# A transformer block on one core: one ring of Q and K for row maxima and logits, and a last half tile packed with gate and up

## The reference, cut to what matters

```
x  = x + layernorm(attn(layernorm(x)))
x  = x + layernorm(ffn(layernorm(x)))

attn: q, k, v = h @ Wq, h @ Wk, h @ Wv        # rotary on q and k
      attn = softmax(where(causal, q @ k.T, -1e9) / 8)
      out  = (attn @ v) @ Wo
ffn:  W = NF4[codes] * scales                  # for gate, up and down
      out = (silu(x @ Wg.T) * (x @ Wu.T)) @ Wd.T
```

## Time and profile before

| | |
|---|---|
| median of three runs | 2897.58 us |
| the profiled execution | 2898.06 us |
| span of its records | 2896.3 us |
| PE busy | 2703.1 us (93%) |
| DVE busy | 2119.8 us (73%) |
| ACT busy | 1815.4 us (63%) |
| POOL busy | 605.2 us (21%) |
| granted TensorE clock, mean | 0.98 |

### The profile page before, as it was taken

How to read it: one execution, slowest core, us unless ns; L and a number is a source line. 1 busy time by engine, 2 the same in 40 slices (tenths; PEclk the granted TensorE clock), 3 DMA queues, 4 the chain that set the end, 5 groups by cost and what they waited for, 6 DMA issues and landing times. The chain is left out here.

```text
span 2896.3 us, 54385 instructions
## 1 busy us (share of the span) xinstructions
PE 2703.1 (93%) x19792; PEld 1477.9 (51%) x19792; DVE 2119.8 (73%) x3538; ACT 1815.4 (63%) x2467; POOL 605.2 (21%) x399
## 2 busy tenths in 40 slices
PE   3999999989999999859979999999999999999996
PEld 1544444458888888725534444444444444444442
DVE  6975666568777878336657887887788788788886
ACT  3713334369999999822247767676766767776652
POOL 0100000068888888801120000000000000000011
PEclk9999999989999999979989999999999999999998
DMA  4353322143232332032211111111111111111124
GB/s 146 112 171 109 80 82 72 52 131 81 61 81 65 82 82 68 6 120 84 88 58 55 49 52 52 52 52 51 53 44 52 52 52 52 52 52 48 55 82 166
DMA packets 88664, 213.83 MB, mean 74 GB/s; under 512 B 14032, under 2 KB 18512, under 8 KB 88144
## 3 DMA queue, kind: packets, MB, share of 16 engines
q1 hardware_dynamic: 88400, 210.36, 23.8%
HBM read 174.59 MB, written 35.72 MB: 73 GB/s over the span
## 5 line engine op out<-in xcount | busy, mean ns | idle before, releaser
L1509 PE MATMUL gp<-region,wgu 128*128 128x512 f16 x4224 | 919.7, 380 | 5.9 <-DVEq L1609 3.3
L435 ACT ACTIVATE dequant<-dequant,offsets 128x512 f32<-128x512 f32 x992 | 659.3, 713 | 89.6 <-DVE dequant L464 45.6
L1509 PEld LDWEIGHTS gp<-region,wgu 128*128 128x128 f16 x4224 | 413.5, 98 | 507.2 <-issue 11.4
L966 POOL TENSOR_TENSOR pt_pair<-probs,pt_pair 128x1024 f16<-128x1024 f32 (+1 forms) x256 | 522.9, 2073 | 117.7 <-ACT probs L1113 117.4
L1524 PE MATMUL yp<-wd,inter 128*128 128x512 f16 x2112 | 465.6, 380 | 17.2 <-DVE wd L482 10.5
L290 DVE TENSOR_REDUCE mx<-sx 128x1 f32<-128x512 f32 (+3 forms) x640 | 363.3, 604 | 87.8 <-PE sx L280 57.0
L390 POOL TENSOR_TENSOR st<-st,eps 128x1 f32<-128x1 f32 x64 | 24.4, 381 | 1751.5 <-DVE st L1217 1511.0
L1108 ACT ACTIVATE pt_pair<-st,coef 128x1024 f16<-128x1024 f32 (+1 forms) x320 | 321.8, 1006 | 58.1 <-PE st L1035 53.8
L464 DVE TENSOR_TENSOR dequant<-dequant 128x512 f32<-128x512 f32 x496 | 341.1, 688 | 10.0
L1524 PEld LDWEIGHTS yp<-wd,inter 128*128 128x128 f16 x2112 | 205.9, 98 | 271.5 <-DVE wd L482 13.0
L806 PE MATMUL pq<-region,ht 128*128 128x512 f16 x1536 | 338.0, 379 | 3.0 <-DVEq L858 3.0
(11 more groups left out here) (123 smaller groups left out, 3256.7 us busy)
## 6 DMA issues: line engine op xcount, KB each, us to landing
qk_pairs<-r_pair SPq DMA_DIRECT2D x128, 128.0 KB, 2.3
k<-qk_pairs SPq DMA_DIRECT2D x48, 256.0 KB, 5.3
dequant<-in_down_codes SPq DMA_DIRECT2D x44, 256.0 KB, 3.0
dequant<-in_down_scales SPq DMA_DIRECT2D x88, 128.0 KB, 3.2
dequant<-in_gate_codes SPq DMA_DIRECT2D x40, 256.0 KB, 2.9
dequant<-in_gate_scales SPq DMA_DIRECT2D x80, 128.0 KB, 3.1
dequant<-in_up_codes SPq DMA_DIRECT2D x40, 256.0 KB, 2.9
dequant<-in_up_scales SPq DMA_DIRECT2D x80, 128.0 KB, 3.2
```

Source lines behind the costliest of these rows:

```text
L435: a.activation(line[:, k % 4, :], code7, ACT.Identity, scale=slope, bias=offsets[:, k:k + 1]).then_inc(s_L.sem, 1)
L966: eng.tensor_tensor(pt_pair[:, n0(u, g) % PT_RING, 1, 0:w], probs[:, n0(u, g) % P_RING, 0:w], pt_pair[:, n0(u, g) % PT_RING, 0, 0:w], ALU. ...
L1509: mm = pe.matmul(gp[:, e % 2, m, :], wgu[par][:, m, a, col0:col0 + P], xnT[:, b, k, tok], start=(k == 0 and a == b), stop=(k == KT - 1 and ...
```

## The change

It has three parts.

1. **Attention.** `q1`, `k1` and the two slots of `xq`, `xk` become one ring of three slots, head mod 3, which the maxima and the logits both read. The whole of head 0 is readied in the Q and K block: its maxima as before, and now also `turn_max`, the conversion (`shifted`), `spread_max`, and the loads of `q2`, `k2`; the three small operations for `shift` move there too, and POOL writes the constant rows of `k2[0]` there. SP's wait for the last stores moves into the attention block, behind the load of head 1's ring slot; POOL waits for them as well before it writes the constant rows of `k2[1]`. The attention block begins with the logits of head 0 (y = 28); the maxima of head 1 begin at y = 30, with 4 in the first slot and 3 in each of twelve more, those of head 2 take 17 slots (3, 2, 2, ...), the others two per slot as before. A head's ring slot is loaded when the logits of the head three before it are done.
2. **The packed half tile.** In the last group the second tile has only 64 real units. Its 64 gate and 64 up columns are placed side by side in one tile, so `gate_up` of that tile is 24 matmuls and not 48, and its `down` takes 2 matmuls and not 3 (the high and the low half of the product lie in the two halves of the partitions). The group before writes gate and up weights in this layout (`short_places`, up units with two instructions each on ACT and DVE); two of the down units are loaded twice over (`doubled`). ACT copies the gated half tile twice. The loop has one turn less: groups 8, 9 and 10 are straight code.
3. **GpSimd's addition of x1.** `output` moves from DVE to POOL, x1 has a ring of four rows loaded three ahead, and the scaled rows `yn` lie in a buffer of the dequantisation that is free by then.

```diff
+        RING = 3
+        FIRST_SLOTS = [4] + [3] * 12
+        SECOND_SLOTS = [3, 2, 2] * 5 + [3, 2]
...
+        y = XLEAD + 2
+        for head in range(1, HEADS):
+            counts = {1: FIRST_SLOTS, 2: SECOND_SLOTS}.get(head, [len(p) for p in per_slot])
+            k = 0
+            for n in counts:
+                maxima_in[y] = [(head, i) for i in range(k, k + n)]
+                k, y = k + n, y + 1
+            turn_in[y] = head
...
-            for y in range(NGH, last_lag):
-                slot(look(0, y))
-            for t in range(HEADS // 2):
-                for y in range(last_lag, last_lag + PAIR):
-                    slot(look(t, y))
+            for y in range(XLEAD, XLEAD + LAG_PV + HEADS * NGH):
+                slot(y, at_slot(y))
...
+                load_ring(sp, 1)
+
+                for u in range(2):
+                    sp.wait_ge(d_qk.sems[u], d_qk.done(KT))
+                load_low(sp, 1)
+                for head in range(HEADS):
+                    if head:
+                        spread_max(sp, head)
                         sp.wait_ge(s_S.sem, s_S.room(head * NGH))
+                    if head + 2 < HEADS:
+                        load_ring(sp, head + 2)
+                    if head and head + 1 < HEADS:
+                        load_low(sp, head + 1)
...
-            with eng.Fori(0, (NG - 1) // 2) as it:
+            with eng.Fori(0, (NG - 3) // 2) as it:
                 for par in range(2):
-                    body(it * 2 + par, par, False)
-            body(NG - 1, (NG - 1) % 2, True)
+                    body(it * 2 + par, par, False, False)
+            for g in range(NG - 3, NG):
+                body(g, g % 2, g == NG - 1, g == NG - 2)
...
+                            if last and t == 1:
+                                for k in range(KT):
+                                    col0 = k * GW + P
+                                    for a, b in ((0, 0), (0, 1), (1, 0)):
+                                        mm = pe.matmul(gp[:, 1, 0, :], wgu[par][:, 0, a, col0:col0 + P],
+                                                       xnT[:, b, k, tok], start=(k == 0 and a == b),
+                                                       stop=(k == KT - 1 and a == 1))
+                                mm.then_inc(s_u.sem, 1)
+                                continue
...
+                                    if last and t == 1:
+                                        for b in range(2):
+                                            mm = pe.matmul(yp[:, d % 4, :], inter[:, c % 2, 0, 1, j * P:(j + 1) * P],
+                                                           wd[:, b, E + n * CH:E + (n + 1) * CH],
+                                                           start=False, stop=(b == 1))
+                                        continue
...
+                for i in range(ST):
+                    pool.wait_ge(s_var6.sem, s_var6.done(i))
+                    inverse_root(pool, st6[:, i % 2, :], s_eps6, s_root6, i)
+                    if i:
+                        output(i - 1)
+                output(ST - 1)
```

More of the change, by code:

```diff
@@ L284, in piece, with maximum @@
             mm.then_inc(s_X.sem, 1)
-        def maximum(v, banks, head, u, k):
+        def maximum(v, banks, head, k):
             qt, c = items[k]
@@ L417, in dequant_buffers, with load_unit @@
             return cst, sst, line, below, above, code7
-        def load_unit(sp, buffers, n, slot, m, g, q):
+        def load_unit(sp, buffers, n, slot, m, g, q, doubled=False):
             cst, sst = buffers[0:2]
@@ L423, in load_unit @@
             cols = slice(q * CH, (q + 1) * CH)
+            if doubled:
+                for half in range(2):
+                    rows = slice(half * BLOCK, (half + 1) * BLOCK)
+                    sp.dma_start(cst[rows, slot, :], codes[m][g, 0:BLOCK, cols]).then_inc(d_st.sems[slot], 16)
+                sp.dma_start(sst[:, slot, :], scales[m][g:g + 1, 0, cols].to_broadcast([P, CH])
+                             ).then_inc(d_st.sems[slot], 16)
+                return
             sp.dma_start(cst[:, slot, :], codes[m][bass.ds(g, 1), :, cols].rearrange("a p c -> p (a c)")
@@ L790, in _ @@
                                 sp.wait_ge(d_qk.sems[which], d_qk.done(1))
-                            load_max(sp, 0, 0)
-                for u in range(2):
-                    sp.wait_ge(d_qk.sems[u], d_qk.done(KT))
+                            load_ring(sp, 0)
+                            load_low(sp, 0)
+                        if (t, u) == (KT - 1, 0):
+                            spread_max(sp, 0)
+            @block.gpsimd
+            def _(pool):
+                pool.memset(k2[0][D:P, :], GUARD).then_inc(s_guard.sem, 1)
             @block.tensor
@@ L1015, in slot @@
                         low_halves(pool, *z)
-                slots(pool, slot)
+                slots(slot)
             @block.tensor
@@ L1081, in times_v, with slot @@
                         mm.then_inc(s_PV.sem, 1)
-                def slot(at):
-                    x, turn, z, w = at(0), at(1), at(XLEAD), at(XLEAD + LAG_PV)
+                def slot(y, at):
+                    z, w = at(XLEAD), at(XLEAD + LAG_PV)
                     if z:
                         scores(*z)
-                    if turn and turn[2] == NGH - 1:
-                        turn_max(turn[0], turn[1])
-                    todo = per_slot[x[2]] if x else []
+                    if y in turn_in:
+                        turn_max(pe, sx, turn_in[y])
+                    todo = maxima_in.get(y, [])
+                    first = (len(todo) + 1) // 2
                     for half in range(2):
-                        if half < len(todo):
-                            item(x[0], x[1], todo[half])
+                        for head, k in todo[first:] if half else todo[:first]:
+                            item(head, k)
                         if w:
@@ L1095, in _ @@
                 pe.wait_ge(s_unset.sem, s_unset.done(1))
-                pe.wait_ge(s_guard.sem, s_guard.done(1))
-                slots(pe, slot)
+                slots(slot)
             @block.scalar
@@ L1558, in weight_high @@
                             a.wait_ge(s_u.sem, s_u.done(g * EVS + (-1)))
+                        if short_next and r >= UNITS:
+                            for unit, hi, _ in short_places(r, par):
+                                op = a.activation(hi, unit, ACT.Copy, scale=col(wfac, G_ + m))
+                            op.then_inc(s_whi.sem, 1)
+                            return
                         a.activation(hi_out, work[3][:, r % 2, :], ACT.Copy, scale=col(wfac, G_ + m)
@@ L1607, in _, with body @@
             def _(v):
[L1608 removed]
+                for s in (s_it, s_ilo, s_add):
                     v.sem_inc(s.sem, s.credit)
[L1610 removed]
+                def body(g, par, last, short_next):
                     def add(c, k):
```

327 lines of the change are left out of this document (176 added, 151 removed).

## The result

| | before | after |
|---|---|---|
| median of the runs | 2898.61 us (4 runs) | 2878.68 us (4 runs, 2877.71 to 2880.70) |
| ratio, 95% interval | | 0.9932 (0.9920 to 0.9944) |
| the profiled execution | 2898.06 us | 2877.71 us |
| span of its records | 2896.3 us | 2875.9 us |

The account below looks back on a forecast made before the run. It took ACT's exponentials to set attention's pace and PE's matmuls the feed-forward block's. Gains of 13.3 + 3.3 + 16.9 = 33.5 us turned 2898.06 into 2864.6, predicted as a 2864.1 us median, range 2854 to 2878 (8 in 10).

Parts of the forecast that it names:

- The start: Border of Q and K block and attention: first logits at about 582.4 instead of 600.50, 18.1 us gained.
- Attention: 18.1 - 3.5 - 0.8 - 0.5 = 13.3 us gained: Attention: border gain less head 1's maxima (3.5), head 2's maxima (0.8) and the wait for head 1's load (0.5).
- most of that overlaps, and I add 0.8: Slots with head 1's maxima: DVE's 28.1 us plus 0.8 for waits on PE, 28.9 us for 13 slots.
- Rival 1: Attention: interleaved maxima not hidden at all, 10.5 us come back instead of 3.5; 2871.1 us, chance 12%.
- The loop turn: Feed-forward loop, group 8 as straight code: no issue stall or late unit at its start, 3.3 us gained.
- The last group: Feed-forward's last group: 149.8 - 6.6 - 10.3 = 132.9 us, 16.9 less.
- the sixth tile: Last group: the sixth tile's result comes 86.9 us from the group's start, a gain of 6.6 us.
- the pause: Last group: PE pauses some 8 us for the fourth down unit, until 43.1 us from the group's start.
- packing: Last group: removed matmuls gain 6.6 us up to the sixth tile; doubled copies cost 1.2, waiting for gated tile 7 0.5.
- The addition on POOL: Last group's rows: 9.1 us leave DVE's path, 3.0 gained at the last row, 1.4 lost waiting for the inverse root.
- the earlier loads of x1: Last group's rows: waits for x1 go because it is loaded three rows ahead, 4.3 us for the last, 1.3 for others.
- Rivals 2 to 4: Last group: POOL's addition delays DVE's factors (10%, 2876.1); dequantisation keeps up (6%, 2854); POOL and DVE exclude each other (5%, 2907).

Follow-up runs that it names:

- e5: Changed kernel plus one 128x1 tensor_tensor on POOL in the Q and K block: whole kernel gained 4.3 us.
- e3: Changed kernel with PE's three pieces of maxima spread over the slot: first exponential of head 0 to that of head 3 is 2.1 us shorter.
- e7: Changed kernel with early tensor_tensor on POOL and spread maxima, loads unchanged: first exponential of head 0 to that of head 3 is 10.2 us shorter.
- e4: Changed kernel with spread maxima and later loads of heads 1 and 2: 2869.3 us.
- e6: Changed kernel with early tensor_tensor on POOL, spread maxima and later loads of heads 1 and 2: median 0.4% below the changed kernel.
- e9: Changed kernel without the packed half tile, straight code and POOL's addition kept: last group 9.2 us longer.
- e10: e9 with the loop's five turns again: feed-forward start to last group 1267.0 us against 1264.6; medians 0.6 us apart.
- e8: Changed kernel with x1 added on DVE again, ring of four rows kept: last group 6.3 us longer, median 5.3 us longer.
- e1: Changed kernel with low halves of head 1 and ring slot of head 2 loaded later: POOL's first subtraction at 593.59 us, before 595.10.

## Why the prediction was wrong

- **The start, right in size.** 18.1 us forecast, 17.4 measured, 17.8 like with like.
- **The step that failed: "Attention: 18.1 - 3.5 - 0.8 - 0.5 = 13.3 us gained".** The sum has no term for POOL. I took the wait and the 16 maxima ahead of the logits for pure loss, and asked only what of PE and DVE they held up. They were also the cover of POOL's preparation. In its place the runs show a wait of 9.07 us on POOL that holds up ACT for 7.0. The early operation takes it away: 4.4 us in stage A alone (e5), 8.1 with the maxima spread (e3 to e7). The row that would have told was one that I did not use: POOL's first subtraction with 17.1 us of waiting, the first `tensor_tensor` after a reduction over partitions. Its like could be seen elsewhere: POOL's rows contain 23.3 us of idle time put down to issue, and they stand in one piece ahead of the very first of these operations, which also follows a reduction over partitions (23.50 us in the changed kernel). The Trainium skill (GPSIMD Engine Reference, section Instruction dispatch) says that the first call to a freshly loaded kernel costs a load of about 6 us "with no visible profile instruction". The trace agrees that no record shows it; the time here is longer, 6.9 us (e4) to 11.7 us (e6). That the wait here is such a load is not shown.
- **The second: "most of that overlaps, and I add 0.8".** This term was mis-sized. DVE's sum of 28.1 us for 13 slots was a fair floor, but PE and DVE share two buffers, and with two pieces side by side each waits for the other (8.1 us of DVE and 2.0 of PE from 600 to 625). From group 3 to group 15 the changed kernel took 628.03 - 598.25 = 29.8 us, e7 617.45 - 590.67 = 26.8. The forecast for these twelve slots was 28.9 x 12/13 = 26.7: it was right for the pieces spread and wrong for the order that the kernel had. The pace depends on where in PE's slot the pieces stand, which I had read in the code and not priced. Rival 1 had the place right; it had 7 us more coming back than the forecast, and of the 10.9 us that came back too much about 4.4 lie there.
- Both together are 10.2 of the 10.9 us by which more came back than in the sum; e7 has 5.5 us coming back where the prediction had 4.8. The two are not additive: the hole hid some maxima and left PE at the low clock, so each fix alone shows little (4.4 and 2.1).
- **The loop turn**: 3.3 forecast, 2.2 measured in stage B, and 2.4 by e9 against e10. Group 8 gained 2.2 us (124.6 against 126.8) and group 7, the last of the loop, 0.9 at its end, together near the forecast; but group 9 takes 125.4 us where it took 124.3. There PE waits 0.85 us for DVE's addition into `y_rows` in the middle of the first `down` (the row at 2664.75). e9 has the same 125.4 without any unit in two instructions, so these are not the cause; why DVE is late there was not found.
- **The last group, right in size by luck.** 133.4 against 132.9, with the sixth tile at 86.9 as forecast, although the pause was 0.7 us longer and what came behind it 0.7 shorter. Behind the sixth tile the terms do not hold one by one. By the prediction's terms packing is worth 6.6 - 1.2 - 0.5 = 4.9 us; e9 shows 9.2. The addition on POOL is 6.4 by the terms (9.1 + 3.0 - 1.4, less the 4.3 us of waiting for x1 in that 3.0, which e8 does not bring back); e8 shows 6.3. For the earlier loads of x1 the terms have 1.3 + 4.3 = 5.6, and of the 16.4 us measured 0.9 are left for it (an estimate; no run has the old ring). A part of the difference can be seen in the wait of DVE for PE at the last tile, 4.62 us in e9: a DVE that is done sooner waits longer there, unless packing makes PE sooner too. So packing was undersized by about what the loads of x1 were oversized. POOL's addition took 2.35 us (forecast 2.13).
- **Rivals 2 to 4 did not happen.** With POOL adding 2.35 us in each row the row stayed at 3.42 us, so DVE's factors and statistics do not wait for it. PE's pause of 9.03 us says that the dequantisation does not keep up. What does exclude each other is seen in e8: POOL's 0.19 us operation takes 1.10 us beside DVE's addition of two operands, and ends with it.

In sum: 33.5 us forecast against 20.4 in the profiled execution; 11.5 of the 13.1 missing lie in attention, 1.1 in the loop, 0.5 in the last group.

## What to carry to other kernels

When a wait is removed, list what every engine, also the idle ones, was getting done under it. An engine's long idle time ahead of its first operation of a kind can hold a preparation that has no record (here POOL's first `tensor_tensor` after a reduction over partitions); a single tiny operation of that kind in an earlier idle stretch took it out of the way. And where two engines hand small pieces over through two buffers, spread the pieces over the slot, one between each two longer works, before judging by the engines' sums. Two such faults can mask each other: try the fixes together as well as apart.

## What the hardware showed unexpectedly

POOL's unrecorded wait took 9.07 us with the DMA engines full (share 1.0 until 594), 9.2 to 9.3 in e8, e9 and e10, 9.90 in e3, and 8.02 and 6.93 with later loads (e1, e4). In the Q and K block it took 10.65, 11.71 and 11.06 us (e5, e6, e7), and there too the DMA engines were busy at first (in e5 a share of 0.86 to 1.03 from 234 to 240); whether their traffic stretches it was not tested apart. The profile names the wait only as issue; that an instruction stands there can be read in the listing alone. From the first projection matmul to the first exponential the changed kernel and its edits take one of two times 1.7 us apart (351.3 and 353.0 us), and nothing in the edits goes with it; what does was not found.
